# Turning the quantised x on TensorE directly behind the self scores, ahead of the turned cross attention

## The reference, cut to what matters

```
x = x + attn(layernorm(x), Wq, bq, Wk, bk, Wv, bv, Wo, bo)             # 16 heads of 32, rotary, causal
x = x + xattn(layernorm(x), ctx, wq, bq, wkv, bkv, wp, bp)             # int8 fake-quantised q and output projections
x = x + ffn(layernorm(x), router_w, w_gate, w_up, w_down)              # 64 experts, top 8, silu(gate) * up, down

def _qdq(x):   # symmetric, per row, along the last axis
    s = jnp.maximum(jnp.max(jnp.abs(x), axis=-1, keepdims=True) / 127.0, 1e-08)
    return jnp.clip(jnp.round(x / s), -127.0, 127.0) * s

# inside xattn
q = _qdq(x) @ _qdq(wq).T + bq
k, v = jnp.split(cond @ wkv.T + bkv, 2, axis=-1)
attn = jax.nn.softmax(jnp.einsum('bnhd,bmhd->bhnm', q, k) * scale, axis=-1)
o = jnp.einsum('bhnm,bmhd->bnhd', attn, v)
out = _qdq(o) @ _qdq(wp).T + bp
```

## Time and profile before

| what | value |
|---|---|
| timed runs | 1784.63, 1784.66, 1791.47 us |
| profiled execution | 1771.08 us |
| its span, first to last instruction | 1769.2 us |
| TensorE matmul busy | 1480.6 us (84%) |
| VectorE busy | 1165.4 us (66%) |
| ScalarE busy | 966.9 us (55%) |
| GpSimd busy | 674.6 us (38%) |
| mean granted clock of TensorE | 0.918 of full speed |

### The profile page before, as it was taken

How to read it: one execution, slowest core, us unless ns; L and a number is a source line. 1 busy time by engine, 2 the same in 40 slices (tenths; PEclk the granted TensorE clock), 3 DMA queues, 4 the chain that set the end, 5 groups by cost and what they waited for, 6 DMA issues and landing times.

```text
span 1769.2 us, 36416 instructions
## 1 busy us (share of the span) xinstructions
PE 1480.6 (84%) x11380; PEld 1111.3 (63%) x11380; DVE 1165.4 (66%) x3111; ACT 966.9 (55%) x3345; POOL 674.6 (38%) x654
## 2 busy tenths in 40 slices
PE   3699988888898888988888888888872988887895
PEld 2577766666666666766666666666651655555564
DVE  6788776777777777767767777776762444444453
ACT  3477665666666666666666666666661433333342
POOL 0114333333334333433333433333343355444465
PEclk9899999998999999999899999999985999999997
DMA  9752222221110101000001010100049799999974
GB/s 299 285 203 97 90 90 101 100 85 61 44 40 28 36 24 30 24 24 24 24 24 30 24 32 27 30 24 19 19 133 331 209 274 273 278 247 301 267 132 50
DMA packets 159930, 196.01 MB, mean 111 GB/s; under 512 B 39733, under 2 KB 121909, under 8 KB 159872
## 3 DMA queue, kind: packets, MB, share of 16 engines
q1 hardware_dynamic: 120960, 157.47, 27.1%
q0 software_dynamic: 38912, 37.87, 10.5%
HBM read 127.80 MB, written 130.29 MB: 146 GB/s over the span
## 4 chain that ended last, share of the span: by engine, by line
DVE 25%; PE 22%; DMA 20%; issue 14%; another core or an unknown queue 12%; ACT 5%; POOL 1%; DVEq 1%; SPq 0%; POOLq 0%
DMA out<-x,slots 18%; PE bank L513 11%; PE bank L519 4%; DVE small L1250 3%; ACT probs L980 3%; PE bank L541 3%; DVE xn L1269 2%; DVE wide_a L1319 2%; DVE small L1283 2%; PE bank L495 2%; DVE small L1273 1%; DVE x L1325 1%; DVE x L1450 1%; DVE wide_b L1493 1%
## 5 line engine op out<-in xcount | busy, mean ns | idle before, releaser
L980 ACT ACTIVATE probs<-bank,small 128x128 f32<-128x128 f32 x1024 | 364.2, 384 | 155.5 <-DVE small L1283 152.1
L1732 POOL TENSOR_TENSOR small<-small,half 128x1 f32<-128x1 f32 x96 | 54.6, 568 | 721.5 <-DVE small L1255 719.9
L1767 POOL DMA_INDIRECT routed<-row,slots x248 | 252.9, 1020 | 132.6 <-issue 72.9
L1836 POOL DMA_INDIRECT out<-x,slots x128 | 200.1, 1563 | 202.2 <-DMA out<-x,slots 148.5
L1283 DVE TENSOR_REDUCE small<-bank 128x4 f32<-128x512 f32 x256 | 166.9, 684 | 133.1 <-remote 125.1
L980 ACT ACTIVATION_READ_ACCUMULATOR probs<-bank,small 128x1 f32 x1024 | 228.6, 223 | 0.0
L974 ACT ACTIVATE probsT<-bank 128x512 f32<-128x512 f32 x256 | 144.0, 610 | 84.3 <-PE bank L541 81.9
L541 PE MATMUL bank<-idf,probs 128*128 128x128 f32 x1024 | 160.4, 293 | 3.9 <-ACT probs L980 3.9
L541 PEld LDWEIGHTS bank<-idf,probs 128*128 128x128 f32 x1024 | 130.5, 152 | 35.4 <-issue 6.5
L513 PE MATMUL bank<-w_q_hi,xT_hi 128*128 128x512 f32 x128 | 73.5, 575 | 79.3 <-DVE xatt L1299 35.7
L1687 DVE TENSOR_SCALAR slots<-pairs 128x1 uint32<-128x1 f32 x128 | 13.7, 149 | 189.3 <-DMA out<-x,slots 182.9
(11 more groups left out here) (242 smaller groups left out, 3982.5 us busy)
## 6 DMA issues: line engine op xcount, KB each, us to landing
w_gate_up<-in_w_gate SPq DMA_DIRECT2D x128, 192.0 KB
w_gate_up<-in_w_up SPq DMA_DIRECT2D x128, 192.0 KB
w_down<-in_w_down SPq DMA_DIRECT2D x128, 192.0 KB
routed<-empty_row SPq DMA_DIRECT2D x16, 1280.0 KB, 10.1
x_in<-in_x SPq DMA_DIRECT2D x32, 256.0 KB, 2.6
ctx_sb<-in_ctxT_in SPq DMA_DIRECT2D x32, 256.0 KB, 3.0
x_res<-in_x SPq DMA_DIRECT2D x32, 256.0 KB, 2.6
out<-x SPq DMA_DIRECT2D x32, 256.0 KB
```

The source lines that it names most:

```text
L980: last = act.activation(probs[:, g, j * P:(j + 1) * P], bank[:, b, j * P:(j + 1) * P], ACT.Exp, bias=negated[:, h:h + 1], **({"accum_out": ...
L1732: pool.tensor_tensor(c["r0"], c["v"], half[:, :], ALU.pow).then_inc(g_pow[kind], 1)
L1767: pool.indirect_dma_start(routed, bass.IndirectOffsetOnAxis(ap=slots_of(m)[:, k:k + 1], axis=0), row_of(m)[:, :], None, bounds_check=SLOTS ...
L1836: pool.indirect_dma_start(out.rearrange("b p (h c) -> (b p h) c", h=2), bass.IndirectOffsetOnAxis(ap=place_of[k % 2][:, half_:half_ + 1], ...
```

## The change

`turn_quantised_x` is called directly behind `self_scores`, ahead of `turn_cross_attention`, instead of between the first and the second third of the cross value product. Since it now comes before the wait for `e_oT` in TensorE's order, it gets that wait of its own (for tile m - 1 in its counting, which is the same tile as cur - 4 in the other call). The three parts of the cross value product follow one another without a break.

```diff
             def turn_quantised_x(m):
                 reached(pe, d_q8, m, 5, 5)
+                reached(pe, e_oT, m - 1, 1, 1)
                 turn_bf16(5, xq8, p_q8T)
...
                 if has(cur - 2):
                     self_scores(cur - 2)
+                if has(cur - 3):
+                    turn_quantised_x(cur - 3)
                 if has(cur - 4):
                     turn_cross_attention(cur - 4)
                 if has(cur - 3):
                     cross_values_b(cur - 3)
-                if has(cur - 3):
-                    turn_quantised_x(cur - 3)
                 if has(cur - 3):
                     cross_values_c(cur - 3)
```

## The result

| | kernel before | with the change |
|---|---|---|
| timed, median (range) of 9 runs each | 1788.01 (1784.63 to 1791.89) us | 1797.66 (1795.03 to 1801.04) us |
| profiled execution; its span | 1771.08; 1769.2 us | 1801.04; 1799.1 us |
| TensorE matmul busy; mean granted clock | 1480.6 us; 0.918 | 1454.7 us; 0.917 |
| the 26 iterations of the loop | 1051.6 us, 40.45 each | 1072.8 us, 41.26 each |

The change makes the kernel slower by 0.56%: the ratio is 1.0056, with a 95% interval from 1.0041 to 1.0071. That is 9.7 us above the kernel before and 10 us above my 1787.5. The profiled executions are 30 us apart, because the one of before was 17 us shorter than its median and the one of after 3 us longer.

The account below looks back on a forecast made before the run. It took TensorE's late signals during GpSimd's scatters, with the waits before `queries_a` and `keys_a`, to bound the kernel. Terms: 1784.66 + 0 + 2.1 (loop, once) + 0.5 (pipeline's end) = 1787.3, given as 1787.5 us; range 1750 to 1808.

Parts of the forecast that it names:

- What bounds the kernel: In the loop, TensorE's signals come 4 to 7 us late during GpSimd's scatters; TensorE pauses 3.00 and 0.47 us.
- The wait for the quantised x: TensorE's wait ahead of the cross attention's turn costs 0 in the loop, with 0.7 us of cover.
- The order of the signals: Held TensorE signals leave one behind the other: cross attention's comes 2.9 us later, turned x's 2.9 us earlier.
- the sixth place: Cross attention's new place among TensorE's held signals, between 835.65 and 838.58; the upper end was taken, 2.9 us later.
- my second rival: Sixth signal comes with the fifth, average hardly later, no gap before `keys_a`: 1743 us, chance 0.30.
- What the later signal costs: In the loop, 2.9 us later costs 1.0 us, given back; loop stays 26 x 41.0, plus 2.1 us once.
- settling: Loop iterations return to 41.0 us by the clock's raster, with the clock back at +13.2; lengths around 41.5 would refute it.
- slower rival: Loop iterations don't return to 41.0 us but take 41.87 each: 1808 us, chance 0.27 (0.28 by the time's class).
- faster rival: Sixth signal comes with the fifth, iterations nearly like the 39.39 us one from 790.44: 1743 us, chance 0.30.
- slope of 0.49: In the loop, each us of low clock adds 0.49 us of iteration length, from 0.73/1.5.
- pipeline's end: Last iteration with a quantised x: cross attention is turned behind x, 0 to 1.0 us later; 0.5 us taken.
- likeliest case: Whole kernel: loop iterations stay at 41.0 us, time 1787.5 us, own range 1781 to 1797, chance 0.38.

Follow-up runs that it names:

- the last occasion: Changed kernel, last 4 of 8 scatters meant to wait for the turned x's copy (edit did nothing): 1540.9 us, ratio 1.0068 to the unedited kernel before's 1530.2.
- the kernel with one score signal: Kernel before, with one signal behind all self scores and one behind all cross scores instead of four each: 1781.59 us, ratio 1.0059.
- attention-first kernel: Kernel before, with x turned directly behind the cross attention's turn and the value products in one run: 1760.84 us, ratio 0.9947.
- in halves: Kernel before, first 4 of a tile's 8 scatters at the old place, last 4 only after the turned x is copied: 1644.0 us, ratio 0.9213.
- before, paced: Kernel before, each scatter issued only when the one before it has landed: 1913.8 us, ratio 1.0726 to the kernel before.
- after, paced: Changed kernel, each scatter issued only when the one before it has landed: 1910.2 us, ratio 1.0704 to the kernel before.

## Why the prediction was right or wrong

*What bounds the kernel.* Right as a reading, and not enough as a cause. Leaving out the scatters, pacing them and moving them each took the contested signals' delay away on its own occasion. But the last occasion shows that scatters back to back are not enough for it: there the same code ran at 1530 us.

*The wait for the quantised x, priced at 0.* Right where signals are held: there the scores are issued later than x is ready, and in no row of the changed kernel above does TensorE wait for VectorE there. Wrong where they aren't: 0.24 to 0.37 us per iteration, 10.0 us without scatters and 10.7 us on the last occasion. The cover that I read at 829 goes with the disturbance: there x is finished 1.0 us ahead of the cross attention's turn, without scatters 0.3 us behind it. The scores' matmuls have pauses in the one (0.24 us) that they lack in the other. The added wait for `e_oT`, priced at 0 too, cost nothing: in the changed kernel's trace the turns of x (L500) wait for VectorE and never for ScalarE.

*The order of the signals* is the step that failed, in one half. The cross attention's signal comes later by about what I said (+8.0 to +8.7 in all but one iteration, instead of mostly +5.8), and the turn itself stands 0.2 to 0.8 us further behind the scores, where I had put 0.2. The turned x's does not come 2.9 us earlier, and its copy has 2.08 us of idle time where I wanted next to none. In nearly all iterations both leave in one burst, 0.06 us apart. The upper end that I took for the sixth place was right: in the kernel before, the product's signal, which is the sixth, is raised at +8.67, with the seventh. But I had thought of places in a row; the kernel with one score signal showed that the count doesn't matter. The Trainium skill, page "TensorE: Matmul & The Clock Gate", section "The cost: per-tile semaphore tail", has increments follow one another in program order some 26 ns apart. The trace agrees on the order, and inside the burst (0.06 us apart) and on the last occasion (the scores' signals 0.04 us apart) its spacing is of that size, though longer; the rule says nothing of the hold ahead of the burst. The spacing of my second rival, the sixth signal with the fifth, was thus right, but both came at the late place, and the gain that it gave to that spacing didn't follow.

*What the later signal costs.* I had put the loop at 26 x 41.0 in either kernel and 2.1 us once. In the profiled changed kernel iterations are 41.05 to 41.07 from 274 to 438, then between 39.4 and 42.6, and 41.26 on average: 6.8 us above 26 x 41.0. I had named lengths that vary around 41.5 as the sign against settling; they vary, around 41.2. The slower rival (41.87 each) is not what happened, and neither is full settling. The price of the faster rival rested on a misreading: the iteration from 790.44 restarts at +7.6, later than the usual +6.9. It is short because its clock is low for 3.4 us and not for 6.8. The slope of 0.49, which I took from it and an unlike one, holds between like ones: back at +12.8 the iteration from 185.40 takes 39.79 us, back at +15.2 the one from 428.72 takes 41.00, which is 0.50.

*What was missing* is the iteration ahead of the loop, 5.6 us. I had looked only at the loop and the pipeline's end, for which I added 0.5 us and the profiles show 0. In the timed runs the difference is 9.7 us. With the 6.4 us that the profile shows ahead of the loop, some 3 us would be left for the rest, near to my 2.6; but the timed runs can't be divided, so this sum is argued and not shown. The attention-first kernel divides the change more safely: the one run of value products -0.5%, x ahead of the cross attention +1.1%. The sum also started from three runs, 1784.66 us; from the median of nine, 1788.01, it gives 1790.6, and 7 us of the 10 are left.

The range held the time, but it is wide, its upper end came from a rival that didn't happen, and the 1781 to 1797 that I gave the likeliest case just missed. Of the chances, 0.28 for slower was too little. Two costs of the same size, one with the hold and one without, make the change slower by 0.6 and 0.7%, and I had priced the one at 2 us and the other at nothing; that they are alike is chance.

What stays open: how GpSimd's scatters hold TensorE's signals at all, what differs between an occasion on which signals are held and one on which they aren't, what decides which signal passes, and how much of the kernels' gain in halves (not run on an occasion without the hold) is left there. If no signal is held there, I would expect none.

## What to carry to other kernels

Where a wait has no sender in the trace and the sending engine is long done, look at what another engine was issuing at that time, and run the kernel once without it: here that one run showed 244 us. Do so on more than one occasion; on another those 244 us weren't there. A cover that such a disturbance provides is no cover; price an added wait also as if the disturbance were gone. A signal that others wait for stands ahead of one that nobody misses, and a reordering is checked at every edge of a hardware loop, not only in it.

## What the runs showed of the hardware that I had not expected

- While GpSimd issued its 8 indirect DMAs 0.3 us apart, signals of TensorE's matmuls were raised 3 to 8 us late on every occasion but the last; with 1.9 us or more between them none was late at the contested place. VectorE's signal to TensorE was prompt meanwhile (L1299 over at 836.63, TensorE on at 836.68).
- Held signals were raised in TensorE's order and in groups, 0.04 to 0.06 us apart within one; the last group came 1.1 to 1.3 us behind the end of the last scatter in the kernel before.
- On another occasion the same unedited kernel took 1530 us instead of 1770 to 1790, and the changed kernel's trace from it has its scatters just as close together. A ratio measured on one occasion holds for that condition.
- Iterations of quite different content took 40.96 us (before, paced), 40.92 (after, paced) and 40.91 to 41.01 (one score signal, from 834 to 1203) again and again, each with one stretch of low clock in it; with the cross queries turned three times they didn't.
